# The recurrence's step: magnitude power and magnitude as one exponential of a joined exponent

## The reference, cut to what matters

```python
def step(h, inp):
    x_t, dt_t, B_t, C_t, xr_t = inp
    h_carrier = h.mean(axis=1)
    T = jnp.cos((c_phase(xr_t) - c_phase(h_carrier)) / 2.0) ** 2
    alpha = jnp.exp(dt_t[..., None] * A_neg)
    expo = 1.0 + (1.0 - alpha) * KAPPA * (1.0 - T[:, None, :])
    mag, ph = (c_mag(h), c_phase(h))
    cmag = jnp.minimum(jnp.exp(expo * jnp.log(mag + 1e-08)), 10.0)
    h = from_polar(cmag, ph)
    Bx = B_t[:, None, :, :] * (dt_t * x_t)[:, :, None, None]
    h = h + Bx
    h = from_polar(jnp.tanh(c_mag(h)), c_phase(h))
    y_t = jnp.einsum('bnc,bdnc->bd', C_t, h)
    return (h, y_t)
```

## Time and profile before

| | us |
|---|---|
| median of 3 runs | 13085.5 |
| lowest, highest | 13085.5, 13089.1 |
| span of the profiled execution | 13078.4 |
| VectorE busy | 9955.2 (76%) |
| ScalarE busy | 8368.0 (64%) |
| TensorE matmul busy | 5746.3 (44%) |

### The profile page before, as it was taken

How to read it: one execution, slowest core, us unless ns; L and a number is a source line. 1 busy time by engine, 2 the same in 40 slices (tenths; PEclk the granted TensorE clock), 3 DMA queues, 4 the chain that set the end, 5 groups by cost and what they waited for, 6 DMA issues and landing times. The chain is left out here.

```text
span 13078.4 us, 218367 instructions
## 1 busy us (share of the span) xinstructions
PE 5746.3 (44%) x52526; PEld 4265.9 (33%) x52542; DVE 9955.2 (76%) x54539; ACT 8368.0 (64%) x42451; POOL 94.6 (1%) x164
## 2 busy tenths in 40 slices
PE   5222222222222222222222222222227978888998
PEld 5222222222222222222222222222224546753335
DVE  5777777777777777777777777777773957968874
ACT  6666666666666666666666666666663733254666
POOL 0000000000000000000000000000000100000000
PEclk8555555555555555555555555555557988998999
DMA  1000100001000000000010000100000000001100
GB/s 55 14 14 14 21 14 14 14 14 20 14 14 14 14 17 17 14 14 14 14 20 14 14 14 14 20 14 14 14 14 14 1 13 16 1 27 56 30 23 21
DMA packets 339443, 227.40 MB, mean 17 GB/s; under 512 B 27662, under 2 KB 324183, under 8 KB 337884
## 3 DMA queue, kind: packets, MB, share of 16 engines
q1 hardware_dynamic: 338140, 213.30, 7.6%
HBM read 187.41 MB, written 25.43 MB: 16 GB/s over the span
## 5 line engine op out<-in xcount | busy, mean ns | idle before, releaser
L533 PE MATMUL scan_p_car<-scan_hs,scan_mean_mat 32*32 32x2 f32 x16392 | 578.3, 198 | 6837.1 <-DVE scan_hb L660 6824.1
L533 PEld LDWEIGHTS scan_p_car<-scan_hs,scan_mean_mat 32*32 32x32 f32 x16392 | 401.5, 135 | 7016.7 <-DVE scan_hb L660 7003.6
L578 ACT ACTIVATE scan_act_ps<-scan_act_ps 128x64 f32<-128x64 f32 (+1 forms) x8193 | 1642.6, 200 | 64.6
L578 ACT ACTIVATE scan_act_ps<-scan_r 128x64 f32<-128x64 f32 x2048 | 466.2, 228 | 1873.2 <-DVE scan_r L657 1873.2
L560 PE MATMUL scan_p_y<-scan_c_masked,scan_hb 128*64 128x4 f32 x16384 | 1234.5, 253 | 0.0
L538 PE MATMUL scan_p_car<-scan_eps_row,ones 1*128 1x3 f32 x4102 | 1198.0, 360 | 39.3 <-DMA scan_a_log<-L_attn_a_A_log 39.1
L578 ACT ACTIVATE scan_cm<-scan_dl,scan_s 128x64 f32<-128x64 f32 x2049 | 712.0, 347 | 729.6 <-DVE scan_s L683 729.6
L657 DVE TENSOR_TENSOR scan_c<-scan_V,scan_cm 128x64 f32<-128x64 f32 x4096 | 738.1, 221 | 470.1 <-ACT scan_cm L578 425.3
L560 PEld LDWEIGHTS scan_p_y<-scan_c_masked,scan_hb 128*64 128x64 f32 x16384 | 1055.4, 216 | 34.8
L538 PEld LDWEIGHTS scan_p_car<-scan_eps_row,ones 1*128 1x128 f32 x4102 | 1020.2, 307 | 72.1 <-DMA scan_a_log<-L_attn_a_A_log 39.5
L660 DVE SCALAR_TENSOR_TENSOR scan_uw<-scan_w,scan_rsq 128x64 f32<-128x64 f32 x2048 | 459.5, 224 | 660.3 <-ACT scan_rsq L578 654.7
(11 more groups left out here) (450 smaller groups left out, 17413.5 us busy)
## 6 DMA issues: line engine op xcount, KB each, us to landing
scan_step_in<-scan_scratch SPq DMA_DIRECT2D x520, 256.0 KB, 6.0
qk_scratch<-qkv_parts SPq DMA_DIRECT2D x32, 384.0 KB, 2.5
attn_qT<-qk_scratch SPq DMA_DIRECT2D x192, 64.0 KB, 2.2
attn_kT<-qk_scratch SPq DMA_DIRECT2D x192, 64.0 KB, 2.2
scan_scratch<-prep_dts SPq DMA_DIRECT2D x32, 256.0 KB, 2.1
x<-L_attn_a_x SPq DMA_DIRECT2D x1, 4096.0 KB
out<-x SPq DMA_DIRECT2D x1, 4096.0 KB
filter_in_taps<-c_kT SPq DMA_DIRECT2D x1, 2048.0 KB
```

What stands on the lines that cost most here:

```text
L533: last = nc.tensor.matmul(p_car[slot][rows, 0:2], mean_mat[rows, :], hs[rows, :], start=False, stop=True)
L578: nc.scalar.activation(dst, src, func, **kw).then_inc(counts[par]["act"], 1)
```

## The change

The exponential is taken of the whole exponent, so that the magnitude itself no longer stands as a factor. With be = 1.25 - alpha/4 and am = alpha - 1, the exponent is y = lm*be + lm*am*dot*rs, and C = Exp(y) is the new magnitude. V is the state's direction alone, `hb * ru`. In the step:

- `am` and `be` are new, two tensor_scalar operations with constants on VectorE behind `bx`, and wait for `alpha`.
- `y2` = lm*be, `dd` = (lm*dot)*am and `y` = (dd*rs)+y2 stand in place of `dl`, `F` and `s`; `dd` and `y` are scalar_tensor_tensor operations whose scalar (`dot`, `rs`) is a [128,1] tile.
- `C` = Exp(y) has no scale of its own and stands in place of `cm`.
- `V` waits for `ru` and stands behind `y`.
- `mag` is written to PSUM instead of SBUF; it is now read by `lm` alone.

```diff
-DVE_STEP = [... "dot", "dl", "F", "s", "V"]
+DVE_STEP = [... "bx0", "bx1", "am", "be", "uw0", ... "dot", "y2", "dd", "y", "V"]
...
-        lr, E2, ln2 = (act_ps[0][:, q * J:(q + 1) * J] for q in range(3))
+        lr, E2, ln2, mag = (act_ps[0][:, q * J:(q + 1) * J] for q in range(4))
...
-                    after(act, "dve", "s", par, k)
-                    op(par, cm[:, :], dl[:, :], ACT.Exp, scale=s_[:, 0:1])
+                    after(act, "dve", "y", par, k)
+                    op(par, C[:, :], y[:, :], ACT.Exp)
...
                     after(dve, "act", "lm", par, k)
-                    stt(sem, dl[:, :], alpha[:, (k + 1) % 2, :], 1.0, lm[:, :], ALU.subtract, ALU.mult)
+                    tt(sem, y2[:, :], lm[:, :], be[:, :], ALU.mult)
+                    after(dve, "dve", "dot", par, k)
+                    stt(sem, dd[:, :], lm[:, :], dot[:, 0:1], am[:, :], ALU.mult, ALU.mult)
+                    after(dve, "act", "rs", par, k)
+                    after(dve, "dve", "dd", par, k)
+                    stt(sem, y[:, :], dd[:, :], rs[:, 0:1], y2[:, :], ALU.mult, ALU.add)
                     after(dve, "act", "ru", par, k)
-                    stt(sem, F[:, :], mag[:, :], EPS_MAG, ru[:, :], ALU.add, ALU.mult)
-                    after(dve, "act", "rs", par, k)
-                    after(dve, "dve", "dot", par, k)
-                    nc.vector.tensor_scalar(s_[:, :], rs[:, :], dot[:, 0:1], -0.25, ALU.mult, ALU.add).then_inc(sem, 1)
-                    after(dve, "dve", "F", par, k)
-                    tt(sem, V[:, :, :], hb[:, slot, 0:2, :], F[:, :].unsqueeze(1).to_broadcast([P, 2, J]), ALU.mult)
+                    tt(sem, V[:, :, :], hb[:, slot, 0:2, :], ru[:, :].unsqueeze(1).to_broadcast([P, 2, J]), ALU.mult)
+
+                def powers(sem, k):
+
+                    nc.vector.tensor_scalar(am[:, :], alpha[:, (k + 1) % 2, :], 1.0, None, ALU.subtract).then_inc(sem, 1)
+                    nc.vector.tensor_scalar(be[:, :], alpha[:, (k + 1) % 2, :], -0.25, 1.25, ALU.mult, ALU.add).then_inc(sem, 1)
...
                 dve.wait_ge(al_first, 1)
+                powers(powers_first, CS - 1)
+                dve.wait_ge(powers_first, 2)
                 after_state(1, CS - 1, 1)
...
                             b_products(sem, nxt, k_nxt)
+                            after(dve, "act", "al", par, k)
+                            powers(sem, k)
                             if k and k % YS == 0:
                                 output(par, n * CS, k - 1)
```

More of the change, by code:

```diff
@@ L402, in _ @@
                     nc.vector.tensor_tensor(xr[1], xr[1], xrs[:, :], ALU.mult).then_inc(soft_done, 1)
-DVE_STEP = ["c0", "c1", "w0", "w1", "sq0", "sq1", "r2", "n2", "bx0", "bx1", "uw0", "uw1", "h0", "h1", "nh", "hp", "dot", "dl", "F", "s", "V"]
-ACT_STEP = ["al", "l", "M", "ln2", "E", "rsq", "L1", "R", "th2", "l2", "mag", "lnh", "nsq", "lm", "lnn", "ru", "rs", "cm"]
+DVE_STEP = ["c0", "c1", "w0", "w1", "sq0", "sq1", "r2", "n2", "bx0", "bx1", "am", "be", "uw0", "uw1", "h0", "h1", "nh", "hp", "dot", "y2", "dd", "y", "V"]
+ACT_STEP = ["al", "l", "M", "ln2", "E", "rsq", "L1", "R", "th2", "l2", "mag", "lnh", "nsq", "lm", "lnn", "ru", "rs", "C"]
 PE_STEP = ["carrier", "y"]
@@ L449, in scan_phase @@
         c, w, sq, uw, bx, V = (ph.sb(n, [P, 2, J]) for n in ("c", "w", "sq", "uw", "bx", "V"))
-        r2, n2, rsq, R, th2, nh, lm, dl, mag, ru, F, cm = (
-            ph.sb(n, [P, J]) for n in ("r2", "n2", "rsq", "R", "th2", "nh", "lm", "dl", "mag", "ru", "F", "cm"))
+        r2, n2, rsq, R, th2, nh, lm, ru, C = (
+            ph.sb(n, [P, J]) for n in ("r2", "n2", "rsq", "R", "th2", "nh", "lm", "ru", "C"))
+        am, be, dd, y2, y = (ph.sb(n, [P, J]) for n in ("am", "be", "dd", "y2", "y"))
         act_ps = [ph.ps(f"act_ps{k}", [P, 512]) for k in range(2)]
-        lr, E2, ln2 = (act_ps[0][:, q * J:(q + 1) * J] for q in range(3))
+        lr, E2, ln2, mag = (act_ps[0][:, q * J:(q + 1) * J] for q in range(4))
         M, L1, l2, lnh = (act_ps[1][:, q * J:(q + 1) * J] for q in range(4))
@@ L456, in scan_phase @@
         squares, nsq, lnn = act_ps[1][:, 256:259], act_ps[1][:, 260:261], act_ps[0][:, 260:261]
-        dot, s_, rs = (ph.sb(n, [P, 1]) for n in ("dot", "s", "rs"))
+        dot, rs = (ph.sb(n, [P, 1]) for n in ("dot", "rs"))
         p_car = [ph.ps(f"p_car{k}", [P, 512]) for k in range(2)]
@@ L462, in scan_phase @@
         tab_in, mask_in, bx_first, al_first = ph.sem("tab_in"), ph.sem("mask_in"), ph.sem("bx_first"), ph.sem("al_first")
+        powers_first = ph.sem("powers_first")
         y_out, left, cleared, taken = ph.sem("y_out"), ph.sem("left"), ph.sem("cleared"), ph.sem("taken")
@@ L718, in _ @@
                             nxt, k_nxt = following(par, k)
-                            after(dve, "act", "cm", par, k - 1)
+                            after(dve, "act", "C", par, k - 1)
                             after(dve, "dve", "V", par, k - 1)
                             for comp in range(2):
-                                tt(sem, c[:, comp, :], V[:, comp, :], cm[:, :], ALU.mult)
+                                tt(sem, c[:, comp, :], V[:, comp, :], C[:, :], ALU.mult)
                             for comp in range(2):
```

## The result

The changed kernel takes 13407.35 us (median of 4 runs, 13405.2 to 13415.0), the kernel before 13085.59 us (4 runs). The ratio is 1.0245, with a 95% interval from 1.0231 to 1.026: slower by 322 us, where 137 us was forecast and 13330 us was the upper end of the range. The direction was right, the size was not.

What follows compares the result with a forecast made beforehand. The prediction took the kernel as bound by the scan's VectorE-ScalarE chain, 2048 steps of 4.66 us; +0.077 for the later `scan_c` less 0.010 for `mag` gave +0.067 us a step, +137 us, 13223 us; range 13110 to 13330 us, chance 0.76.

Steps and rivals of the forecast that it cites:

- What bounds the kernel: Scan loop: a chain crossing between VectorE and ScalarE counts 2048 times; 0.01 us on it is 20 us of kernel.
- Step 1, `y2`: Start of `y2` after `scan_products`: +0.155 us, between +0.137 (shorter `lm`) and +0.17 (held by the accumulator read).
- Steps 2 and 3, the durations: `dd` and `y` on VectorE: 0.277 us each, 0.225 plus 0.052 for the [128,1] scalar.
- The rivals that hid it: Pointer reads hidden in `dd` and `y`: both, 13010 us, chance 0.12; only `y`'s, 13116 us, chance 0.06.
- the halved rate: Rival: two fp32 sources slow `dd` and `y` by another 0.066 us each, 13493 us; chance 0.01.
- Step 3, "`dd` (0.034 after its end)": Handover from `dd` to `y` on VectorE: `y` starts 0.034 us after `dd` ends, at +0.606; `rs` no longer late.
- Steps 4 to 6: `C` lasts 0.256, first `scan_c` +1.207 against +1.13; `mag` in PSUM takes 0.01 off; `V` covered by 0.09 us.
- The gain of 0.01 from `mag`: ScalarE behind `mag` in PSUM: operations up to `scan_products` move up 0.01 us, bounds 0 and 0.03.
- Step 7, `am` and `be`: VectorE behind `bx`: about 0.10 us each, 0.21 together, hidden in 0.34 idle before `uw0`, 0.24 in 192 steps.
- The rival in which they didn't fit: `am` and `be` take 0.44 us together, `uw0` starts late: +224 us on top, 13447 us; chance 0.05.
- The sum: Whole step: 0.077 - 0.010 = +0.067 us, over 2048 steps +137 us, 13223 us.

Runs made afterwards that it cites:

- e2: Changed kernel with the constant 1.0 instead of `rs` as `y`'s scalar, both waits kept: 13253.6 us, 165 above the kernel before.
- e4: Changed kernel with the constant 1.0 as `dd`'s scalar and `dot` as `y`'s, both waits kept: 13284.0 us, 195 above the kernel before.
- e1: Changed kernel with the two waits before `y` swapped, `dd` (late) first, then `rs`: 13234.8 us, then 13240.3 us (4 runs), ratio 1.0123.
- b5: b3 with ScalarE's carrier squares ahead of `lnh` and `rs` ahead of `ru`: 13029.9 us, ratio to the kernel before 0.9958.
- b1: Kernel before with the two waits ahead of the first `scan_c` swapped, `V` first, `cm` (late) last: 13216.1 us, 139.5 above before.
- b3: Kernel before with `mag` in PSUM, `s` ahead of `F`, `V` cut in two, `cm`'s wait last before `scan_c`: 13029.8 us, ratio 0.9965.
- b4: b3 with the two waits before the first `scan_c` turned round, `cm` first, first `V` last: 13057.9 us, ratio to the kernel before 0.9984.
- e3: Changed kernel with the wait on `rs` before `y` left out and `dot` as `y`'s scalar: 13217.6 us, 129 above the kernel before.

## Why the prediction was wrong in size

*What bounds the kernel.* Right. The whole difference lies in the recurrence's chain, and every hundredth on it counted 20 us.

*Step 1, `y2`.* It started at 0.13, below even the early end of 0.137: `lm` shrank to 0.236, and the accumulator read did not hold its successor.

*Steps 2 and 3, the durations.* `dd` 0.279 and `y` 0.285, against 0.277. The [128,1] scalar costs 60 ns, where 52 was forecast, shown by e2 (285 to 225) and e4 (279 to 219) with a constant in its place. The rivals that hid it fall, and so does the halved rate: with a constant, `y` takes 225 ns with two fp32 tensors.

*Step 3, "`dd` (0.034 after its end)".* This is the step that failed. The price came from `r2` and its successor, which has a single wait. `y` has two, and its late one is last in the code; the gap is 0.117. The missing term is 0.083 us a step, 170 us in all; taking it away (e1) gave 161 us. It stands in none of the bounds: my own range allowed for a dearer scalar, but for no cost of the wait. The rows that I read from the kernel before don't have this form, with the late wait last: `scan_c` names `cm` first. I should have noticed that I was using a single-wait row for a two-wait instruction. The trace of the kernel before does have the form elsewhere. `nh` names first the state's real part (`h0`, ready 0.02 earlier) and then `th2`, the late one, and this is its timeline just ahead of the earlier trace rows:

```profile
4004.15 0.26 ACT L578 ACTIVATE scan_th<-scan_R 128x64 f32<-128x64 f32 x1
...
4004.51 0.22 DVE L660 SCALAR_TENSOR_TENSOR scan_nh<-scan_hb,scan_th 128x64 f32<-128x64 f32 x1
```

`th2` ends at 4004.15 + 0.256 = 4004.41, and `nh` starts 0.10 later, in this step and in the median of all. That price was there to be read before anything was run.

*Steps 4 to 6.* `C` at 0.256 was right, and `V` stayed covered. The gain of 0.01 from `mag` did not come: from its start to that of `scan_products` it is 0.51 now and was 0.50. b5 shows how little there is to be had by an earlier place in ScalarE's queue: 0.03 at the squares and 0.013 at `scan_products`, with `lnh` moved behind them.

*Step 7, `am` and `be`.* 186 and 187 ns each. The 0.34 of idle time before `uw` is the usual step (0.336); the quotient that the prediction gives for it, 654.7 / 2048, is 0.32, the mean with the 192 steps in it. The idle time fell to 244.5 / 2048 = 0.12 on the mean, 0.132 in the usual step and 0.035 in the 192, and `uw` still starts 0.033 after `rsq` has ended, in every step. The rival in which they didn't fit falls.

*The sum.* With the waits exchanged (e1) the kernel takes 13240 us, 161 above the kernel before (146 in the first, single run); the forecast was 137. In the usual step e1 stands at 4.700 us against 4.633, which is the 0.067 of the forecast. That it fits so closely is partly luck, for the small misses cancel: `y2` started 0.02 earlier than forecast, while `dd`, `y` and the steps between them were 0.01 longer and `mag`'s 0.01 did not come. The other 23 us of e1 are the single long steps (42 us of them, 19 before), for which the sum had no term and whose cause stays open. In the changed kernel the loop's 328 us are thus 137 of the forecast, 0.081 x 2048 = 166 of the wait and 25 of the long steps.

## What to carry to other kernels

Where a VectorE instruction waits for two events, write the one that arrives last first in the code, so that it is built into the instruction; here that was worth 1.2% of the kernel. The sign of it is a start 0.10 us or more after the late event instead of 0.034. At `y` the profile named no releaser for that idle time, at `scan_c` in b1 it named the late event. The start was never earlier than about 0.034 after the built-in wait's event and 0.10 after the separate wait's, so the order is worth at most 0.07 to 0.08 us a time, and only as much as the two events lie apart: where they were 0.01 apart (b3 and b4), it was worth 0.01. In a chain that is repeated thousands of times, price a handover from a row with the same number and order of waits, not only the same engines.

## What the runs showed of the hardware

- A wait held by a separate instruction starts the next one 0.10 to 0.12 us after the event, one held by the instruction itself 0.033 to 0.037. The first consists of 0.037 to 0.039 to the separate instruction's start, its 0.021, and 0.045 (0.055 with a [128,1] scalar) to the next one's start. A wait already met costs little when it is the separate one (e1 against e3: 0.037 and 0.036). All of this is VectorE.
- A [128,1] scalar on a 128x64 scalar_tensor_tensor costs 60 ns of duration (0.279 and 0.285 against 0.219 and 0.225), whether the instruction was queued (`dd`) or had waited (`y`). For ScalarE's Exp it is 0.347 against 0.256.
- ScalarE's `lm`, reading `mag` from PSUM instead of SBUF, is 30 ns shorter at 64 columns (266 to 236), and so is `ru` behind it (267 to 237), whose source did not move. This alone makes the kernel before 0.5% faster.
